# Graph network on one core: the direct products move to the node update's PSUM bank, builds get a fourth bank and their one-hots a third slot

## The chip, the cores and the metric

The kernel runs on 1 core of one Trainium2 chip. The metric is the device time of that core in microseconds; the median of several executions is compared. Before the change it is 2679.72 us (3 runs, 2676.95 to 2680.86).

## The reference

Two layers of message passing over a graph of 6250 nodes with 64 features and 206250 edges, which are sorted by target `dst`; every node has a loop to itself.

```
h  = relu(layernorm(x))
m  = relu(concat(h[src], edge_attr) @ W1 + b1) @ W2 + b2        # per edge
a  = segment_sum(m, dst)
x  = x + relu(concat(h, a) @ U1 + c1) @ U2 + c2                 # the node update
h2 = relu(layernorm(x))
out = x + segment_sum(h2[src] * edge_weight, dst)
```

## The kernel before

The edges come in 202 groups of 1024 (8 tiles of 128). Since they are sorted by target, the targets of a tile span at most 6 nodes and those of a group at most 40 (the kernel tests that and has a slow branch for other graphs, which isn't taken here). The nodes are held as 50 blocks of 125, and 5 blocks are a chunk (10 chunks).

**Pass 1** (`fast_groups`, written out by hand on each engine, one step `s` for a group) does two things with each group.

The first is layer 1. POOL gathers the 128 rows of a tile from `table1` by an indirect DMA (L608, 8 for a group), three groups ahead at most (`gather1` waits for `pre_made` of three groups before). TensorE turns the edge features (`turn_ea`, L916) and multiplies them (`make_q`, L923). DVE adds the gathered rows to the product (`add_product`, L1305), makes a one-hot of the targets (`make_hot`, L1310) and adds the sums of the group before to the running sums (`add_sums`, L1318). ACT applies relu (L713), and TensorE sums over the targets (`sum_hid`, L929).

The second prepares layer 2. For each tile TensorE builds a matrix with a row for each node of a block and a column for each of 50 blocks times 6 targets, in which the edge weights stand: a product of two one-hots, the weight split in three bf16 parts (`build_tile`, 3 matmuls of 128x300, L946). DVE makes the one-hots for four tiles at once (`make_quad`, two for a group): one comparison (L1323), four comparisons (L1325) and three multiplies (L1329). Both sides have slots: `hot_eq`, `hot_w` and `hot_key` are there twice, so quad `q` waits until the tiles of quad `q - 2` are built (`tile_built >= 4 (q - 1)`). The products lie in three PSUM banks (`build_bank`, tile `i` waits for `tile_kept` of tile `i - 3`), from which ACT copies them to `tiles` in SBUF (L721, four slots of a group each). DVE makes `make_quad(2s + 2)` and `make_quad(2s + 3)` in step `s`, after `add_product(s)`, `make_hot(s)` and `add_sums(s - 1)`.

A finished group goes to DRAM (SP, L470), and **pass 2** reads it back in pieces of two groups and one or two chunks (`load_piece`, L490) and multiplies it by `h2` (`multiply`, L1032), a batch of two groups after the other (101 batches). The result of a batch is copied by ACT (`keep_u`, L778) and put in its place.

Not all of it waits for pass 2. As soon as the sums of a chunk are complete, its node update is made within pass 1. `SUMMED[c]`, 23 to 202, is the step for it: `make_g` in two halves (L973) in steps SUMMED and SUMMED + 1, `make_up` (L980) in SUMMED + 2, and layer norm on DVE and ACT up to SUMMED + 5. From step `READY[c] = SUMMED[c] + 6` on `h2` of the chunk is known, and batches still to be built multiply it at once (`direct`, L960, half a batch a step, two steps behind). `ready_for(b)` says how many chunks batch `b` takes so. Their sum goes from ACT (`keep_partial`, L729) to DRAM (L476), and their blocks needn't be stored or read again. The direct products have a PSUM bank of their own (`u_bank[0]`); the node update uses `mid_bank`.

Pass 2's loads on SP start when the last `direct_kept` and all stores have landed (`fast_end`).

Of the kernel before, what the change touches and what calls it, by code (L numbers as in the profile page):

```python
# [5 lines left out]
ALU = mybir.AluOpType  # L6
# [8 lines left out]
P = 128  # L15
D = 64
T = 8
# [4 lines left out]
NP = 125  # L22
BLK = 5
# [5 lines left out]
ROUND = 12582912.0  # L29
SLACK = 31.0  # L30
STAGE = 4
SPLIT = 3
PIECES = 10
SLOTS = 4
# [77 lines left out]
def build(nc, x, src, dst, edge_attr, edge_weight, w1, b1, w2, b2, u1, c1, u2, c2, out):  # L112
# [20 lines left out]

    per_group = N * GE / E
    SUMMED = [min(GROUPS, -int(-(CN * (c + 1) + SLACK) // per_group) + 1) for c in range(CHUNKS)]
    READY = [SUMMED[c] + 6 for c in range(CHUNKS)]

    def ready_for(b):

# [20 lines left out]
    with ExitStack() as ctx:  # L160
        def sb(name, shape, dt=F32):
            return ctx.enter_context(nc.sbuf_tensor(name, shape, dt))
# [72 lines left out]

        QW = 2 * P
        KW = 2 * KEYS
        bld = sb("bld", [P, 2 * (QW + PARTS * QW + KW)])
        bld_bf = bld[:, :].bitcast(BF16)
        assert 2 * GROUPS * T <= 2 * (QW + PARTS * QW + KW) and PIECES * 4 * BLK * GC <= STAGE * ROW  # L240

        def quad(at, n):
            return bld_bf[:, 2 * at:2 * at + 4 * n].rearrange("p (e t) -> p e t", t=4)

        hot_eq = [quad(s * QW, P) for s in range(2)]
        hot_w = [[quad(2 * QW + s * (PARTS * QW + KW) + k * QW, P) for k in range(PARTS)] for s in range(2)]
        hot_key = [bld_bf[:, 2 * at:2 * at + 4 * KEYS].rearrange("p (t c) -> p t c", t=4)
                   for at in (2 * QW + PARTS * QW, 2 * QW + 2 * PARTS * QW + KW)]
# [395 lines left out]
        def _(act):  # L644
# [70 lines left out]
            def keep_tile(g, t):  # L715
                i = g * T + t
                if t == 0 and g >= STAGE:
                    act.wait_ge(adj_stored[g % STAGE], 16 * (g // STAGE))
                    wait_count(act, direct_done, direct_upto((g - STAGE) // 2))
                act.wait_ge(tile_built, i + 1)  # L720
                act.copy(tiles[:, g % STAGE, :, t * WT:(t + 1) * WT],  # L721
                         build_bank[i % 3][:, 0:KEYS].rearrange("p (h w) -> p h w", w=WT)).then_inc(tile_kept, 1)

            def keep_partial(b):
                n = direct_upto(b)
                act.wait_ge(direct_done, n)
                if n > 2:
                    act.wait_ge(s_stored[n % 2], 16 * ((n - 1) // 2))
                act.copy(s_stage[:, n % 2, :], u_bank[0]).then_inc(direct_kept, 1)  # L729

            def relu_g(c, half):
                cols = (0, SPLIT * NP) if half == 0 else (SPLIT * NP, CN)
# [11 lines left out]
            def fast_groups():  # L744
                act.wait_ge(table_turned, 20)
                keep_eaT(0, 0, ea_bank)
                keep_eaT(1, 1, ea_bank)
                for s in range(GROUPS + 6):
                    if s < GROUPS:
                        for t in range(3):  # L750
                            keep_tile(s, t)
                        make_hid(s, s % TWO)
                        for t in range(3, T):
                            keep_tile(s, t)
                        if s + 2 < GROUPS:
                            keep_eaT(s + 2, s % TWO, ea_bank)
                    if s % 2 == 1 and s >= 3:
                        b = (s - 3) // 2
                        if b < BATCHES and ready_for(b):
                            keep_partial(b)  # L760
                    for c in range(CHUNKS):
                        if s == SUMMED[c]:
                            relu_g(c, 0)
                        if s == SUMMED[c] + 1:
                            relu_g(c, 1)
                        if s == SUMMED[c] + 2:
                            clear_sums(c)
                        if s == SUMMED[c] + 3:
                            square(2)(c, 0)
                        if s == SUMMED[c] + 4:  # L770
                            root(2)(c, 0)

            def keep_u(b):
# [49 lines left out]
        def _(pe):  # L823
# [115 lines left out]
            def build_tile(g, t):  # L939
                i = g * T + t  # L940
                q, u = i // 4, i % 4
                if u == 0:
                    pe.wait_ge(quad_made, q + 1)
                wait_count(pe, tile_kept, i - 2)
                for k in range(PARTS):
                    last = pe.matmul(build_bank[i % 3][:, 0:KEYS], hot_w[q % 2][k][:, :, u], hot_key[q % 2][:, u, :],  # L946
                                     start=(k == 0), stop=(k == PARTS - 1))
                last.then_inc(tile_built, 1)

            def direct(b, half):  # L950

                many = ready_for(b) * BLK
                low, high = (0, many // 2) if half == 0 else (many // 2, many)
                if half == 0:
                    pe.wait_ge(tile_kept, (2 * b + 2) * T)
                    pe.wait_ge(h2_staged, ready_for(b))
                    wait_count(pe, direct_kept, direct_upto(b) - 1)
                slot = 2 * b % STAGE
                for h in range(low, high):
                    last = pe.matmul(half_of(u_bank[0], h), h2[:, h * D:(h + 1) * D], tiles[0:NP, slot:slot + 2, h, :],  # L960
                                     start=(h < 2), stop=(h >= many - 2))
                if half == 1:
                    last.then_inc(direct_done, 1)

            def make_g(c, half):
                cols = (0, SPLIT * NP) if half == 0 else (SPLIT * NP, CN)
                if half == 0:
                    pe.wait_ge(acc_added, SUMMED[c])
                    wait_count(pe, x1_made, c)
                else:  # L970
                    pe.wait_ge(g_staged, 2 * c + 1)
                for w, of in ((u1a, hT), (w2u, acc1)):
                    last = pe.matmul(mid_bank[0:D, 0:cols[1] - cols[0]], w[:, :],  # L973
                                     of[:, c * CN + cols[0]:c * CN + cols[1]], start=(w is u1a), stop=(w is w2u))
                last.then_inc(g_made, 1)

            def make_up(c):
                pe.wait_ge(g_staged, 2 * c + 2)
                for b in range(BLK):
                    last = pe.matmul(mid_bank[0:NP, b * D:(b + 1) * D], t_stage[:, 0, b * NP:(b + 1) * NP],  # L980
                                     u2_s[:, :], start=True, stop=True)
                last.then_inc(up_made, 1)

            def fast_groups():
# [4 lines left out]
                for s in range(GROUPS + 6):  # L989
# [15 lines left out]
                    if 0 <= b < BATCHES and ready_for(b):  # L1005
                        direct(b, s % 2)
                    for c in range(CHUNKS):
                        if s == SUMMED[c]:
                            make_g(c, 0)
                        if s == SUMMED[c] + 1:  # L1010
                            make_g(c, 1)
                        if s == SUMMED[c] + 2:
                            make_up(c)

            def multiply(b):
# [116 lines left out]
        def _(dve):  # L1132
# [186 lines left out]

            def make_quad(q):  # L1320
                g, t = q // 2, q % 2 * 4
                wait_count(dve, tile_built, 4 * (q - 1))
                dve.tensor_tensor(hot_eq[q % 2], iota_lo[:, :, :], over(lo[:, g, t:t + 4], P), ALU.is_equal).then_inc(eq_made, 1)  # L1323
                for u in range(4):
                    dve.tensor_scalar(hot_key[q % 2][:, u, :], iota_key[:, :], key[:, g, t + u:t + u + 1], None,  # L1325
                                      ALU.is_equal)
                dve.wait_ge(eq_made, q + 1)
                for k in range(PARTS):
                    last = dve.tensor_tensor(hot_w[q % 2][k], hot_eq[q % 2], over(part[k][:, g, t:t + 4], P), ALU.mult)  # L1329
                last.then_inc(quad_made, 1)  # L1330

            def add_up(c, up):
# [7 lines left out]
            def fast_groups():  # L1340
                make_quad(0)
                make_quad(1)
                for s in range(GROUPS + 6):
                    if s < GROUPS:
                        add_product(s, s, q_bank)
                        make_hot(s)
# [3 lines left out]
                        if q < 2 * GROUPS:  # L1350
                            make_quad(q)
                    for c in range(CHUNKS):
                        if s == SUMMED[c] + 3:
                            add_up(c, mid_bank[0:NP, 0:BC])
                            centre(2)(c, 0)
                        if s == SUMMED[c] + 4:
                            variance(2)(c, 0)
                        if s == SUMMED[c] + 5:
                            stage_h2(c, 0)

            def put(b):
# [98 lines left out]
```

## Time and profile before

| | |
|---|---|
| median of 3 runs | 2679.72 us |
| profiled execution | 2659.47 us, its span 2657.7 |
| pass 1's gathers | 63.2 to 2203.6 us |
| pass 2 | 2223 to 2657 us |
| busy | PE 77%, DVE 49%, ACT 37%, POOL 64% |
| TensorE's granted clock, mean | 0.888 |

The span is cut into 40 slices, each digit the busy share of one in tenths. POOL's last busy slice is where pass 1 ends. Until there PE, DVE and ACT are busy less than POOL, and each of them waits at some place in every group, so the busy shares alone don't say who sets the pace.

### The profile page before, as it was taken

How to read it: one execution, taken by the hardware profiler on the slowest of the kernel's cores; microseconds unless marked ns; L12 is line 12 of the kernel's file. 1: busy time of each engine (PE TensorE's matmuls, PEld its weight loads, DVE VectorE, ACT ScalarE, POOL GpSimd, SP SyncE). 2: the span in 40 equal slices, each digit the busy share in tenths (PEclk: the TensorE clock that was granted, in tenths of full speed). 3: DMA queues.
4: the chain of work that ended last, by engine and by line, in shares of the span. 5: the costliest groups of instructions: out<-in, count | busy, mean ns of one | idle time of the engine just before them, and what ended most of it. 6: DMA issues, size and time to landing. Idle time of an engine off the chain costs nothing.

```text
span 2657.7 us, 57208 instructions
## 1 busy us (share of the span) xinstructions
PE 2049.9 (77%) x21651; PEld 1747.1 (66%) x21651; DVE 1311.2 (49%) x4334; ACT 974.0 (37%) x2419; POOL 1691.7 (64%) x1659
## 2 busy tenths in 40 slices
PE   5766666777777877777787777877778878999998
PEld 5555555656665666666666666766666767787886
DVE  6655555555555555556555555555555551111122
ACT  3334344444444444444444444444444441000111
POOL 6777777777777777777777777777777771000000
PEclk9988888888888888888888898889899899999998
DMA  3455444454444444334333333333223226999995
GB/s 88 129 169 173 162 159 159 165 171 140 142 140 148 130 132 135 118 119 127 106 109 113 99 97 94 87 94 85 74 74 82 65 62 240 401 377 384 372 350 163
DMA packets 422423, 414.27 MB, mean 156 GB/s; under 512 B 288562, under 2 KB 374178, under 8 KB 416000
## 3 DMA queue, kind: packets, MB, share of 16 engines
q1 hardware_dynamic: 369348, 354.89, 38.6%
q0 software_dynamic: 52064, 53.17, 8.8%
q8 instruction: 176, 2.88, 0.4%
q10 hardware_dynamic: 732, 2.48, 0.4%
q14 instruction: 103, 0.84, 0.1%
HBM read 258.64 MB, written 151.74 MB: 154 GB/s over the span
## 4 chain that ended last, share of the span: by engine, by line
POOL 62%; issue 19%; PE 9%; DMA 8%; DVE 1%; DVEq 0%; SPq 0%; ACT 0%; POOLq 0%
POOL rows L608 62%; DMA stage<-adjacency 7%; PE pair L1032 5%; PE pair L1039 1%; PE pair L1022 1%; PE pair L1045 1%; PE pair L864 1%; DMA x_all<-in_x_dram 1%; PE pair L852 0%; DVEq L1363 0%; PE pair L960 0%; PE pair L1053 0%; DVE nodes L1368 0%; DVE mean L1140 0%; SPq L490 0%
## 5 line engine op out<-in xcount | busy, mean ns | idle before, releaser
L608 POOL DMA_INDIRECT rows<-table,idx x1616 | 1649.4, 1021 | 512.0 <-issue 492.2
L721 ACT COPY stage<-pair 128x300 f32<-128x300 f32 x1616 | 622.3, 413 | 689.8 <-PE pair L946 687.3
L946 PE MATMUL pair<-bld 128*128 128x300 bf16 x4848 | 813.1, 316 | 4.5 <-DVE bld L1329 4.5
L923 PE MATMUL pair<-w1b,rings 128*128 128x128 f32 x1616 | 307.1, 349 | 530.4 <-DVE rings L1305 530.3
L923 PEld LDWEIGHTS pair<-w1b,rings 128*128 128x128 f32 x1616 | 261.2, 246 | 588.3 <-DVE rings L1305 587.9
L946 PEld LDWEIGHTS pair<-bld 128*128 128x128 bf16 x4848 | 552.2, 120 | 134.7 <-DVE bld L1329 7.9
L1329 DVE TENSOR_TENSOR bld<-bld,part 128x512 bf16<-128x512 bf16 x1212 | 432.4, 410 | 0.0
L1323 DVE TENSOR_TENSOR bld<-iota_lo,lo 128x512 bf16<-128x512 f16 x404 | 172.5, 427 | 471.1 <-PE pair L946 468.3
L1325 DVE TENSOR_SCALAR bld<-iota_key,key 128x300 bf16<-128x300 f16 x1616 | 383.5, 300 | 0.0
L1305 DVE TENSOR_TENSOR rings<-rows,pair 128x512 f32<-128x512 f32 x202 | 138.3, 685 | 461.4 <-DMA rows<-table,idx 461.4
L1032 PE MATMUL pair<-stage,h 125*64 125x96 f32 x5870 | 297.4, 253 | 25.0 <-DMA stage<-adjacency 22.2
L929 PEld LDWEIGHTS pair<-hot,rings 128*65 128x65 f32 x3232 | 289.2, 173 | 14.5 <-DVE hot L1310 1.9
L1032 PEld LDWEIGHTS pair<-stage,h 125*64 125x64 f32 x5870 | 259.9, 139 | 52.1 <-DMA stage<-adjacency 38.6
L713 ACT ACTIVATE rings<-rings 128x512 f32<-128x512 f32 x202 | 128.0, 633 | 423.8 <-DVE rings L1305 423.1
L929 PE MATMUL pair<-hot,rings 128*65 128x40 f32 x3232 | 279.8, 256 | 1.7 <-ACT rings L713 1.7
L960 PE MATMUL pair<-stage,h 125*64 125x96 f32 x4230 | 219.9, 250 | 0.4 <-ACT s_stage L729 0.4
L960 PEld LDWEIGHTS pair<-stage,h 125*64 125x64 f32 x4230 | 187.1, 137 | 29.8 <-issue 29.5
L778 ACT COPY bld<-pair 128x96 f32<-128x96 f32 x101 | 24.0, 238 | 363.4 <-PE pair L1032 363.4
L1377 DVE TENSOR_SCALAR bld<-iota,node_off 128x80 f32<-128x80 f32 x101 | 26.2, 260 | 241.7 <-PE pair L1045 241.7
L916 PE MATMUL pair<-ident,rings 128*128 128x128 f32 x808 | 122.2, 274 | 2.4 <-issue 1.7
L708 ACT COPY rings<-pair 128x512 f32<-128x512 f32 x202 | 118.4, 586 | 14.7 <-PE pair L916 9.9
L916 PEld LDWEIGHTS pair<-ident,rings 128*128 128x128 f32 x808 | 98.4, 141 | 5.9 <-issue 2.0
(131 smaller groups left out, 779.3 us busy)
## 6 DMA issues: line engine op xcount, KB each, us to landing
stage<-adjacency SPq DMA_DIRECT2D x270, 480.0 KB, 9.4
rings<-in_edge_attr_dram SPq DMA_DIRECT2D x202, 256.0 KB
adjacency<-stage SPq DMA_DIRECT2D x28, 1200.0 KB
rows<-table,idx POOLq DMA_INDIRECT x1616
adjacency<-stage SPq DMA_DIRECT2D x20, 1080.0 KB
adjacency<-stage SPq DMA_DIRECT2D x20, 960.0 KB
adjacency<-stage SPq DMA_DIRECT2D x20, 840.0 KB
adjacency<-stage SPq DMA_DIRECT2D x20, 720.0 KB
```

The lines of the kernel that those rows point to most:

```text
L608: pool.indirect_dma_start(out=rows[:, slot, t, :], out_offset=None, in_=table, in_offset=bass.IndirectOffsetOnAxis(ap=idx[:, g, t:t + 1], ...
L721: act.copy(tiles[:, g % STAGE, :, t * WT:(t + 1) * WT], build_bank[i % 3][:, 0:KEYS].rearrange("p (h w) -> p h w", w=WT)).then_inc(tile_ke ...
L916: last = pe.transpose(bank[:, a * P:(a + 1) * P], ea_ring[:, slot, a * P:(a + 1) * P], ident[:, :])
L923: last = pe.matmul(bank[:, a * P:(a + 1) * P], eaT[:, slot, a, :], w1b2[:, :], start=True, stop=True)
L929: last = pe.matmul(out[0:m, 0:W], lhs[:, slot, t, 0:m], hot[:, hot_slot, t, :], start=(t == 0), stop=(t == T - 1))
L946: last = pe.matmul(build_bank[i % 3][:, 0:KEYS], hot_w[q % 2][k][:, :, u], hot_key[q % 2][:, u, :], start=(k == 0), stop=(k == PARTS - 1))
L960: last = pe.matmul(half_of(u_bank[0], h), h2[:, h * D:(h + 1) * D], tiles[0:NP, slot:slot + 2, h, :], start=(h < 2), stop=(h >= many - 2))
L1032: last = pe.matmul(half_of(bank, h), h2[:, h * D:(h + 1) * D], held[:, :, h - low * BLK, :], start=(not begun and h < 2), stop=(h >= NB - 2))
L1305: dve.tensor_tensor(pre[:, slot, :, :], rows[:, place % RING, :, :], bank.rearrange("p (t f) -> p t f", f=D), ALU.add).then_inc(pre_made, 1)
L1323: dve.tensor_tensor(hot_eq[q % 2], iota_lo[:, :, :], over(lo[:, g, t:t + 4], P), ALU.is_equal).then_inc(eq_made, 1)
L1325: dve.tensor_scalar(hot_key[q % 2][:, u, :], iota_key[:, :], key[:, g, t + u:t + u + 1], None, ALU.is_equal)
L1329: last = dve.tensor_tensor(hot_w[q % 2][k], hot_eq[q % 2], over(part[k][:, g, t:t + 4], P), ALU.mult)
```

## The change

Three edits go together, all in pass 1.

1. The direct products move from their own bank to the last 96 columns of the node update's bank (`direct_bank` in `pair[1][:, 1]`). They take turns: `make_g` and `make_up` wait for `direct_kept`, and the direct products wait for `g_staged` and `x1_made` in the steps behind. For this the update starts in an odd step (`UPDATE = SUMMED | 1`) and its parts stand two steps apart: halves in UPDATE and UPDATE + 2, `make_up` in UPDATE + 4, `h2` in UPDATE + 7. READY becomes UPDATE + 8, and the loops have GROUPS + 9 steps instead of GROUPS + 6.
2. The bank that is free becomes a fourth one for builds.
3. The one-hots of a quad get a third slot (`QUADS = 3`), so `make_quad(q)` waits for the tiles of quad `q - 3`.

```diff
-    READY = [SUMMED[c] + 6 for c in range(CHUNKS)]
+    UPDATE = [SUMMED[c] | 1 for c in range(CHUNKS)]
+    READY = [UPDATE[c] + 8 for c in range(CHUNKS)]
...
-        mid_bank = pair[1][:, 1, :]
-        build_bank = [pair[2][:, 0, :], pair[2][:, 1, :], pair[3][:, 0, :]]
+        mid_bank = pair[1][:, 1, 0:SPLIT * NP]
+        direct_bank = pair[1][:, 1, 512 - COLS:512]
+        build_bank = [pair[2][:, 0, :], pair[2][:, 1, :], pair[3][:, 0, :], pair[3][:, 1, :]]
+        BUILDS = len(build_bank)
...
-                wait_count(pe, tile_kept, i - 2)
+                wait_count(pe, tile_kept, i - BUILDS + 1)
...
             def direct(b, half):
...
+                for c in range(CHUNKS):
+                    since = 2 * b + 2 + half - UPDATE[c]
+                    if since in (1, 3):
+                        pe.wait_ge(g_staged, 2 * c + (since + 1) // 2)
+                    if since == 5:
+                        pe.wait_ge(x1_made, c + 1)
...
+            def direct_by(s):
+                b = min((s - 3) // 2, BATCHES - 1)
+                return direct_upto(b) if b >= 0 else 0
...
             def make_g(c, half):
+                wait_count(pe, direct_kept, direct_by(UPDATE[c] + 2 * half))
...
             def make_up(c):
                 pe.wait_ge(g_staged, 2 * c + 2)
+                wait_count(pe, direct_kept, direct_by(UPDATE[c] + 4))
...
-                for s in range(GROUPS + 6):
+                for s in range(GROUPS + 9):
...
-                        if s == SUMMED[c]:
+                        if s == UPDATE[c]:
                             make_g(c, 0)
-                        if s == SUMMED[c] + 1:
+                        if s == UPDATE[c] + 2:
                             make_g(c, 1)
-                        if s == SUMMED[c] + 2:
+                        if s == UPDATE[c] + 4:
                             make_up(c)
...
             def make_quad(q):
                 g, t = q // 2, q % 2 * 4
-                wait_count(dve, tile_built, 4 * (q - 1))
+                wait_count(dve, tile_built, 4 * (q - QUADS + 1))
```

The steps of ACT (`relu_g`, `clear_sums`, `square`, `root`) and DVE (`add_up`, `centre`, `variance`, `stage_h2`) move with those of TensorE, and all uses of `% 2` and `% 3` for the slots become `% QUADS` and `% BUILDS`.

## Rows read from the trace of the kernel before

**Rows 1.** The page's chain that ended last, shares of the span by engine.
```profile
POOL 62%; issue 19%; PE 9%; DMA 8%; DVE 1%; DVEq 0%; SPq 0%; ACT 0%; POOLq 0%
```

**Rows 2.** Waits: engine, line, releaser: us in total, times, longest us.
```profile
POOL rows L608 <- issue: 492.2, 1615, 0.3
...
DVE bld L1323 <- PE pair L946: 468.3, 395, 2.4
DVE rings L1305 <- DMA rows<-table,idx: 461.4, 148, 6.0
```

**Rows 3.** The gathers: durations min/median/max in ns; then busy us, mean ns.
```profile
L608 POOL DMA_INDIRECT rows<-table,idx x1616: 940/944/2608, 63.2 to 2203.6; - x180
...
L608 POOL DMA_INDIRECT rows<-table,idx x1616 | 1649.4, 1021 | 512.0 <-issue 492.2 <-DMA table<-h 19.9
```

**Rows 4.** Timeline (start us, us, instruction [idle before]) of DVE and POOL, 946 to 951.
```profile
946.00 0.69 DVE L1305 TENSOR_TENSOR rings<-rows,pair 128x512 f32<-128x512 f32 x1 [1.22 <-DMA rows<-table,idx]
948.32 0.43 DVE L1323 TENSOR_TENSOR bld<-iota_lo,lo 128x512 bf16<-128x512 f16 x1 [0.88 <-PE pair L946]
949.50 1.08 DVE L1329 TENSOR_TENSOR bld<-bld,part 128x512 bf16<-128x512 bf16 x3
...
948.21 0.95 POOL L608 DMA_INDIRECT rows<-table,idx  x1 [0.30 <-issue]
949.47 1.94 POOL L608 DMA_INDIRECT rows<-table,idx  x1 [0.30 <-issue]
```

**Rows 5.** Timeline of DVE and POOL, 1013 to 1015.
```profile
1013.62 1.09 DVE L1329 TENSOR_TENSOR bld<-bld,part 128x512 bf16<-128x512 bf16 x3
...
1013.11 0.99 POOL L608 DMA_INDIRECT rows<-table,idx  x1 [0.30 <-issue]
1014.41 1.12 POOL L608 DMA_INDIRECT rows<-table,idx  x1 [0.30 <-issue]
```

**Rows 6.** Timeline of DVE and POOL, 1825 to 1833.
```profile
1825.65 0.69 DVE L1305 TENSOR_TENSOR rings<-rows,pair 128x512 f32<-128x512 f32 x1 [3.52 <-DMA rows<-table,idx]
1827.97 0.42 DVE L1323 TENSOR_TENSOR bld<-iota_lo,lo 128x512 bf16<-128x512 f16 x1 [1.13 <-PE pair L946]
...
1827.04 0.94 POOL L608 DMA_INDIRECT rows<-table,idx  x1 [0.31 <-issue]
1829.53 1.18 POOL L608 DMA_INDIRECT rows<-table,idx  x1 [0.30 <-issue]
1832.27 1.26 POOL L608 DMA_INDIRECT rows<-table,idx  x1 [0.30 <-issue]
```

**Rows 7.** Timeline of PE, ACT and SP's queue at the end of pass 1.
```profile
2212.50 2.04 PE L960 MATMUL pair<-stage,h 125*64 125x96 f32 x44 [0.42 <-ACT s_stage L729]
2215.60 2.14 PE L960 MATMUL pair<-stage,h 125*64 125x96 f32 x44
2217.78 0.24 ACT L729 COPY s_stage<-pair 128x96 f32<-128x96 f32 x1 [1.51 <-PE pair L960]
2219.62 4.65 SPq L490 DMA_DIRECT2D stage<-adjacency  x9
2223.59 0.75 PE L1032 MATMUL pair<-stage,h 125*64 125x96 f32 x6 [3.23 <-DMA stage<-adjacency]
```

**Rows 8.** Windows: length; busy of PE, PEld, DVE, ACT, POOL; PEclk, DMA share, GB/s.
```profile
2223.00:2600.00 377.00, 354.68 (x6061) 307.64 (x6063) 54.98 (x252) 37.00 (x164) 0.00 (x0) 0.98 1.03 379
```

**Rows 9.** Timeline of DVE, 999 to 1004.
```profile
999.95 0.69 DVE L1305 TENSOR_TENSOR rings<-rows,pair 128x512 f32<-128x512 f32 x1 [1.76 <-DMA rows<-table,idx]
...
1000.96 0.19 DVE L1318 TENSOR_TENSOR nodes<-nodes,pair 65x40 f32 x1
1003.56 0.43 DVE L1323 TENSOR_TENSOR bld<-iota_lo,lo 128x512 bf16<-128x512 f16 x1 [2.42 <-PE pair L946]
```

**Rows 10.** ACT's copy of a batch's result, first and last of two stretches of pass 2.
```profile
L778 ACT COPY bld<-pair x14: 238/238/239, 2230.3 to 2310.6; 128x96 f32<-128x96 f32 x14
...
L778 ACT COPY bld<-pair x11: 238/238/239, 2603.0 to 2626.3; 128x96 f32<-128x96 f32 x11
```

More of the change, by code:

```diff
@@ L31 @@
 STAGE = 4
+QUADS = 3
 SPLIT = 3
@@ L237, in build @@
         KW = 2 * KEYS
-        bld = sb("bld", [P, 2 * (QW + PARTS * QW + KW)])
+        bld = sb("bld", [P, QUADS * (QW + PARTS * QW + KW)])
         bld_bf = bld[:, :].bitcast(BF16)
-        assert 2 * GROUPS * T <= 2 * (QW + PARTS * QW + KW) and PIECES * 4 * BLK * GC <= STAGE * ROW
+        assert 2 * GROUPS * T <= QUADS * (QW + PARTS * QW + KW) and PIECES * 4 * BLK * GC <= STAGE * ROW
         def quad(at, n):
             return bld_bf[:, 2 * at:2 * at + 4 * n].rearrange("p (e t) -> p e t", t=4)
-        hot_eq = [quad(s * QW, P) for s in range(2)]
-        hot_w = [[quad(2 * QW + s * (PARTS * QW + KW) + k * QW, P) for k in range(PARTS)] for s in range(2)]
+        QUAD = QW + PARTS * QW + KW
+        hot_eq = [quad(s * QUAD, P) for s in range(QUADS)]
+        hot_w = [[quad(s * QUAD + (k + 1) * QW, P) for k in range(PARTS)] for s in range(QUADS)]
         hot_key = [bld_bf[:, 2 * at:2 * at + 4 * KEYS].rearrange("p (t c) -> p t c", t=4)
-                   for at in (2 * QW + PARTS * QW, 2 * QW + 2 * PARTS * QW + KW)]
+                   for at in (s * QUAD + (PARTS + 1) * QW for s in range(QUADS))]
         wgt = bld[:, 0:GROUPS * T].rearrange("p (g t) -> p g t", t=T)
@@ L721, in keep_tile @@
                 act.copy(tiles[:, g % STAGE, :, t * WT:(t + 1) * WT],
-                         build_bank[i % 3][:, 0:KEYS].rearrange("p (h w) -> p h w", w=WT)).then_inc(tile_kept, 1)
+                         build_bank[i % BUILDS][:, 0:KEYS].rearrange("p (h w) -> p h w", w=WT)).then_inc(tile_kept, 1)
             def keep_partial(b):
@@ L728, in keep_partial @@
                     act.wait_ge(s_stored[n % 2], 16 * ((n - 1) // 2))
-                act.copy(s_stage[:, n % 2, :], u_bank[0]).then_inc(direct_kept, 1)
+                act.copy(s_stage[:, n % 2, :], direct_bank).then_inc(direct_kept, 1)
             def relu_g(c, half):
@@ L761, in fast_groups @@
                     for c in range(CHUNKS):
-                        if s == SUMMED[c]:
+                        if s == UPDATE[c]:
                             relu_g(c, 0)
-                        if s == SUMMED[c] + 1:
+                        if s == UPDATE[c] + 2:
                             relu_g(c, 1)
-                        if s == SUMMED[c] + 2:
+                        if s == UPDATE[c] + 3:
                             clear_sums(c)
-                        if s == SUMMED[c] + 3:
+                        if s == UPDATE[c] + 5:
                             square(2)(c, 0)
-                        if s == SUMMED[c] + 4:
+                        if s == UPDATE[c] + 6:
                             root(2)(c, 0)
@@ L943, in build_tile @@
                     pe.wait_ge(quad_made, q + 1)
-                wait_count(pe, tile_kept, i - 2)
+                wait_count(pe, tile_kept, i - BUILDS + 1)
                 for k in range(PARTS):
-                    last = pe.matmul(build_bank[i % 3][:, 0:KEYS], hot_w[q % 2][k][:, :, u], hot_key[q % 2][:, u, :],
+                    last = pe.matmul(build_bank[i % BUILDS][:, 0:KEYS], hot_w[q % QUADS][k][:, :, u], hot_key[q % QUADS][:, u, :],
                                      start=(k == 0), stop=(k == PARTS - 1))
@@ L958, in direct @@
                 slot = 2 * b % STAGE
+                for c in range(CHUNKS):
[4 more added lines that the diff above has]
+                        pe.wait_ge(x1_made, c + 1)
                 for h in range(low, high):
-                    last = pe.matmul(half_of(u_bank[0], h), h2[:, h * D:(h + 1) * D], tiles[0:NP, slot:slot + 2, h, :],
+                    last = pe.matmul(half_of(direct_bank, h), h2[:, h * D:(h + 1) * D], tiles[0:NP, slot:slot + 2, h, :],
                                      start=(h < 2), stop=(h >= many - 2))
@@ L988, in fast_groups @@
                 make_q(0, 0, q_bank)
-                for s in range(GROUPS + 6):
+                for s in range(GROUPS + 9):
                     if s < GROUPS:
@@ L1007, in fast_groups @@
                     for c in range(CHUNKS):
-                        if s == SUMMED[c]:
+                        if s == UPDATE[c]:
                             make_g(c, 0)
-                        if s == SUMMED[c] + 1:
+                        if s == UPDATE[c] + 2:
                             make_g(c, 1)
-                        if s == SUMMED[c] + 2:
+                        if s == UPDATE[c] + 4:
                             make_up(c)
@@ L1321, in make_quad @@
                 g, t = q // 2, q % 2 * 4
-                wait_count(dve, tile_built, 4 * (q - 1))
-                dve.tensor_tensor(hot_eq[q % 2], iota_lo[:, :, :], over(lo[:, g, t:t + 4], P), ALU.is_equal).then_inc(eq_made, 1)
+                wait_count(dve, tile_built, 4 * (q - QUADS + 1))
+                dve.tensor_tensor(hot_eq[q % QUADS], iota_lo[:, :, :], over(lo[:, g, t:t + 4], P), ALU.is_equal).then_inc(eq_made, 1)
                 for u in range(4):
-                    dve.tensor_scalar(hot_key[q % 2][:, u, :], iota_key[:, :], key[:, g, t + u:t + u + 1], None,
+                    dve.tensor_scalar(hot_key[q % QUADS][:, u, :], iota_key[:, :], key[:, g, t + u:t + u + 1], None,
                                       ALU.is_equal)
@@ L1328, in make_quad @@
                 for k in range(PARTS):
-                    last = dve.tensor_tensor(hot_w[q % 2][k], hot_eq[q % 2], over(part[k][:, g, t:t + 4], P), ALU.mult)
+                    last = dve.tensor_tensor(hot_w[q % QUADS][k], hot_eq[q % QUADS], over(part[k][:, g, t:t + 4], P), ALU.mult)
                 last.then_inc(quad_made, 1)
@@ L1342, in fast_groups @@
                 make_quad(1)
-                for s in range(GROUPS + 6):
+                for s in range(GROUPS + 9):
                     if s < GROUPS:
@@ L1352, in fast_groups @@
                     for c in range(CHUNKS):
-                        if s == SUMMED[c] + 3:
+                        if s == UPDATE[c] + 5:
                             add_up(c, mid_bank[0:NP, 0:BC])
                             centre(2)(c, 0)
-                        if s == SUMMED[c] + 4:
+                        if s == UPDATE[c] + 6:
                             variance(2)(c, 0)
-                        if s == SUMMED[c] + 5:
+                        if s == UPDATE[c] + 7:
                             stage_h2(c, 0)
```

1 line of the change is left out of this document (added).

## Prediction

> **What bounds the kernel now.** I read the chain of work that ended last first. 62% of it is POOL at L608, the gathers of pass 1, and 19% is "issue" [rows 1]. The waits of POOL come next: before 1615 of the 1616 gathers it sat idle 492.2 us in total and never over 0.3 us at a time [rows 2]. So no gather ever waited for another engine. POOL issues one after the other from 63.2 to 2203.6 us [rows 3], and that stretch is as long as 1616 gathers of 1.02 us with 0.30 between them. The other engines follow. DVE waits 461.4 us for gathered rows and 468.3 us for TensorE's builds [rows 2]. Whatever gives PE, ACT or DVE slack in pass 1 doesn't shorten it; only a shorter gather does.
>
> The gathers' durations hold the one thing that can move. Their median is 944 ns, their mean 1021 [rows 3]: 1649.4 - 1616 x 0.944 = 124 us are stretch, 0.61 us for each of 202 groups. The rows side by side show what stretches them. At 949.47 a gather takes 1.94 us, and at 949.50 DVE begins three L1329 multiplies that last 1.08 [rows 4]. At 1013.62 the same three begin 0.51 us into a gather, and the price is 0.05 in that one and 0.18 in the next [rows 5]. The two builds begun from 1827.97 on cost 0.24 and 0.32 [rows 6]. The price of a four-tile build on DVE thus lies between 0 and 1.0 us, and depends on where in the gather's 1.25 us period it falls. The number of these instructions doesn't change with the edit. Their places do.
>
> After pass 1 two more stages count: the seam to pass 2 [rows 7], and pass 2, where the DMA engines are busy throughout from 2223 to 2600 us (share 1.03, 379 GB/s) [rows 8].
>
> **Part 1: third slot for the one-hots.** `make_quad(2s+2)` waited for tile 3 of the group in hand, which TensorE builds only after `make_q`. It now waits for all tiles of the group before, which are long built. Today the first L1323 starts 2.3 us after its group's L1305 (946.00 to 948.32, 0.88 of it waiting for PE) [rows 4], or 3.6 us (999.95 to 1003.56) where PE is slower [rows 9]. Without the wait it follows L1318, which ends 1.2 us after L1305's start (999.95 to 1001.15) [rows 9]. The second L1323 needs tile 3, which is there at 2.3 to 3.6 us, before DVE asks at 1.2 + 2.45 = 3.65. So nearly all pairs should stand 2.45 us apart, beginning 1.2 us after L1305. DVE's own gain (part of 468.3 us of waiting) is worth nothing, since it then waits longer for rows.
>
> The price of a pair: of the 201 pairs, 99 already stand 2.45 us apart. I took for each of them the stretch of six gathers from the one in which its first L1323 starts, and set it against the place of that start in the gather's period. A start at 0.09 to 0.15 us costs 1.0 (25 pairs; 948.32 lies 0.11 into the gather of 948.21 [rows 4]). At 0.30 to 0.56 it costs 0.14 (15 pairs), at 0.56 to 0.80 0.30 (7), at 0.80 to 1.04 0.58 (16; 1827.97 lies 0.93 into the gather of 1827.04 [rows 6]), at 1.04 to 1.25 0.67 (31), at 0 to 0.09 0.56 (4). The mean over the 99 is 0.625. Then I asked of each of 190 groups where in the period the moment 1.2 us after its L1305 lies: 12 at 0 to 0.09, 6 at 0.09 to 0.15, 17 at 0.15 to 0.30 (one pair there cost 0.30; I take 0.15), 47, 31, 24 and 53 in the four bins behind. The sum is 6.7 + 6.0 + 2.6 + 6.5 + 9.4 + 14.0 + 35.4 = 80.6 us, or 0.424 a group. The dear place loses most of its members, because 1.2 and 2.3 us lie on different sides of the period. The other operations of a group stretch its gathers by some 0.05 us by the same count, and that stays. So 201 x 0.424 + 10 = 95, and 3 for the gathers before the first group, 98 us of stretch where 124 are now: 26 us less. The places are those of today's landings, which the new order shifts as well (a stored group goes out at another moment, and rows behind it land later), so I take two thirds: **-18 us**. Bounds: -40 (every pair at 0.36) and +30 (every pair at 0.70, the price just behind 1.04).
>
> The Trainium skill has a rule for this, "SBUF — State Buffer", section "SBUF: two separate sides": VectorE and GpSimd share a port pair that is an exclusive lock, held for a whole instruction, and descriptors that GpSimd writes wait for it. The rows agree that there is a block (1.94 us at 949.47), but most of L1329's time costs nothing: 404 x 1.05 = 424 us of multiplies go with 124 of stretch. What it would make of the change is the second rival.
>
> **Part 2: fourth build bank.** `build_tile` waits for the tile four back instead of three. ACT's copies and PE's builds aren't on POOL's path: nothing. The cover is PE's wait for rows; if that were gone, this would be a gain and no cost.
>
> **Part 3: shared bank, later node update.** The direct products now wait after each half of the node update, and `make_g` and `make_up` wait for `direct_kept`. Queued behind these waits are the next group's builds and `make_q`, hence `hid`, and DVE's L1305 two steps on. It is at most three waits for each of 10 chunks. POOL sees L1305 only through `pre_made` of three groups before, so two groups of (2203.6 - 63.2) / 202 = 10.6 us stand in between: nothing, up to a delay of some 17 us.
>
> READY moves from SUMMED + 6 to (SUMMED | 1) + 8. From SUMMED = 23, 43, 63, 83, 103, 123, 143, 164, 184 the sum of `ready_for` falls from 423 to 412: one batch later for seven chunks, two for two. Eleven times 5 blocks of 2 groups (240 KB) are stored and read again, and multiplied in pass 2. There a batch takes (2310.6 - 2230.3) / 13 = 6.18 us with 10 chunks to load and (2626.3 - 2603.0) / 10 = 2.33 with 2 [rows 10]: 0.48 for each. 11 x 0.48 = **+5.3 us**. Bytes alone give 11 x 246 KB / 379 GB/s = 7.1; if the late ones hide in PE's own chain it is 4. The extra stores in pass 1 (2.7 MB in 2100 us) cost nothing beside a half idle DMA.
>
> **Part 4: the seam.** Pass 2's loads (2219.62) wait for the last partial product to be kept and stored. Today `make_g` stands between its halves; it moves behind. The halves run from 2212.50 and 2215.60 [rows 7], the second at once behind the first's 2.04: 2214.5 instead of 2215.6, **-1.1 us**. The node update ends about 1 us later, but only the last piece of batch 0 needs it, and that is far behind the first landing at 2223.59. The bounds are -1.1 and +1.
>
> **Sum.** -18 + 5.3 - 1.1 = -13.8 us on the profiled execution (2659.5, span 2657.7): 0.52%. On the median, 20 us above the profiled one, 2679.7 x 0.9948 = 2666.
>
> **Rivals.** A, the forecast: the pairs leave the dear place. 2666, with its own range 2655 to 2675.
> B: the stretch stays what it is. For it: all instructions remain, and half the pairs already stand 2.45 apart without being cheaper than the rest. It is also what the skill's rule gives, where every overlap blocks for its length. Against it are the 25 pairs at 1.0, whose start the edit removes. +5.3 - 1.1 = +4.2: 2684.
> C, slower: pairs begin just before the end of a period. Rows that land 1.4 us after the last gather (late in pass 1, as at 1825.65) put L1323 at about 1.06, where a pair costs 0.7. It decides if the mean pair costs over (124 - 13) / 201 = 0.55. With 0.70 throughout it is 201 x 0.15 = +30, with half of that +15 + 4.2 = +19: 2699. For it: 53 of 190 stand there already by my count, and early traffic that now scatters the landings may thin.
> D, slower: the bank's turns hold up TensorE by more than the two groups, and POOL waits. The waits are short (a copy of 0.24 us [rows 7]); were it 5 us for each of 10 chunks, 2730.
> That the third slot frees nothing, since DVE finds another wait, falls together with B.
>
> **Chances.** A 0.56, B 0.20, C 0.20, D 0.04. The measurement tells apart about 0.2%, 5.4 us: 2674 to 2685 is "same". A gives faster 0.49 and same 0.07; B same 0.12, slower 0.07 and faster 0.01; C and D slower. Faster 0.50, same 0.20, slower 0.30. The range runs from the deeper bound of part 1 (2648) to C at half weight (2697).
>
> **What would show it.** L608's mean falls from 1021 to about 1010 ns at the same median (each 1% is 16 us); L1323's waiting for PE falls from 468 us to under 100, while L1305's waiting for rows grows by as much. A gather of 1.94 us gets rare. POOL's idle stays at 0.3 at most; if not, it is D. The first load of pass 2 comes 1.6 us after the end of the last L729, as now (2217.78 + 0.24 to 2219.62), and L1032 has 110 more records (5980) with pass 2 some 5 us longer. If L608's mean is 1021 again, B; if over 1030, C. The prediction is wrong above all if the starts of L1323 don't fall where today's landings put them.

## The result, and the profile after

The change makes the kernel slower: 2897.68 us (median of 4, 2884.36 to 2918.09) beside 2680.29. The ratio is 1.082, 95% interval 1.0756 to 1.0885. The forecast was 2666 us in a range of 2648 to 2697. The profiled execution took 2918.09 us, its span 2916.3: 258.6 more than the span before.

The waits and the gathers' group of the changed kernel, in the form of [rows 2] and [rows 3] (L617 is L608 of before, L1327 is L1305, L1345 is L1323):

```profile
DVE rings L1327 <- DMA rows<-table,idx: 1183.5, 200, 9.4
...
POOL rows L617 <- issue: 492.2, 1615, 0.3
...
DVE bld L1345 <- PE pair L955: 27.1, 111, 0.7
```
```profile
L617 POOL DMA_INDIRECT rows<-table,idx x1616: 940/944/5042, 63.3 to 2459.4; - x180
...
L617 POOL DMA_INDIRECT rows<-table,idx x1616 | 1904.9, 1179 | 512.1 <-issue 492.2
```

POOL still waits for nobody: 492.2 us in 1615 pieces of at most 0.3, to the digit as in [rows 2]. The median of a gather is still 944 ns. What grew is the busy time, 1649.4 to 1904.9 us. These 255.5 us are all but 3 of the 258.6. By the reckoning of the prediction (1904.9 - 1616 x 0.944) the stretch is now 379 us, where it was 124. The longest gather takes 5.04 us.

Here is one of the long ones. First DVE, then POOL, start and duration in us (L1332 is the one-hot of the targets, L1340 the sums, L1347 and L1351 the comparisons and multiplies of a quad):

```profile
1001.35 0.69 DVE L1327 TENSOR_TENSOR rings<-rows,pair 128x512 f32<-128x512 f32 x1 [2.36 <-DMA rows<-table,idx]
...
1002.47 0.41 DVE L1345 TENSOR_TENSOR bld<-iota_lo,lo 128x512 bf16<-128x512 f16 x1
1002.80 0.91 DVE L1347 TENSOR_SCALAR bld<-iota_key,key 128x300 bf16<-128x300 f16 x4
1003.64 1.08 DVE L1351 TENSOR_TENSOR bld<-bld,part 128x512 bf16<-128x512 bf16 x3
1004.64 0.41 DVE L1345 TENSOR_TENSOR bld<-iota_lo,lo 128x512 bf16<-128x512 f16 x1
1004.98 0.91 DVE L1347 TENSOR_SCALAR bld<-iota_key,key 128x300 bf16<-128x300 f16 x4
1005.81 1.09 DVE L1351 TENSOR_TENSOR bld<-bld,part 128x512 bf16<-128x512 bf16 x3
```
```profile
1002.65 1.19 POOL L617 DMA_INDIRECT rows<-table,idx  x1 [0.30 <-issue]
1004.14 3.58 POOL L617 DMA_INDIRECT rows<-table,idx  x1 [0.30 <-issue]
1008.02 0.94 POOL L617 DMA_INDIRECT rows<-table,idx  x1 [0.30 <-issue]
```

The gather begins at 1004.14, amid the first quad's multiplies. It ends at 1007.72, 0.82 us after the last multiply of the second quad (1006.90). In the kernel before, the gather of 949.47 [rows 4] was caught in the same way, and this is what stood behind its multiplies:

```profile
950.78 0.43 DVE L1323 TENSOR_TENSOR bld<-iota_lo,lo 128x512 bf16<-128x512 f16 x1 [0.20 <-PE pair L946]
951.12 0.92 DVE L1325 TENSOR_SCALAR bld<-iota_key,key 128x300 bf16<-128x300 f16 x4
951.96 1.09 DVE L1329 TENSOR_TENSOR bld<-bld,part 128x512 bf16<-128x512 bf16 x3
```

It ended at 951.41, 0.83 us after 950.58, where the multiplies ended and DVE waited 0.20 us for TensorE. The gather got through in that short wait, and the second quad cost it nothing. In the group shown from the changed kernel no wait stands there: the second L1345 begins 2.17 us after the first, not 2.45, and the gather waits for both quads. Over the whole trace of the changed kernel 83 of the 201 pairs of quads follow each other so; in the other 118 a pause of about 0.24 us is left in the middle. The pause before the first quad is gone in all 201. The 119 gathers of 1.8 us and more hold 292 us of the stretch, and their median end is 0.82 us after the end of an operation, mostly the last multiply of a quad, behind which VectorE paused.

### The profile page after: what moved, and what is told of

Same layout as the page of the kernel before. It is cut to its first block, busy times and chain, and to the rows that moved or that the text cites. A ratio compares the mean times of both kernels' runs of the same rounds, so it can differ in the third digit from the quotient of the medians.

```text
span 2916.3 us, 57246 instructions
## 1 busy us (share of the span) xinstructions
PE 2116.1 (73%) x21649; PEld 1793.8 (62%) x21649; DVE 1284.4 (44%) x4334; ACT 975.8 (33%) x2418; POOL 1947.2 (67%) x1659
## 4 chain that ended last, share of the span: by engine, by line
POOL 65%; issue 17%; DMA 8%; PE 8%; DVE 1%; DVEq 0%; SPq 0%; ACT 0%; POOLq 0%
POOL rows L617 65%; DMA stage<-adjacency 8%; PE pair L1054 4%; PE pair L1061 1%; PE pair L873 1%; PE pair L1067 1%; PE pair L1044 1%; DMA x_all<-in_x_dram 1%; PE pair L861 0%; DVEq L1385 0%; PE pair L1075 0%; SPq L499 0%; PE pair L975 0%; DVE nodes L1390 0%; DVE mean L1162 0%
## 5 line engine op out<-in xcount | busy, mean ns | idle before, releaser
L617 POOL DMA_INDIRECT rows<-table,idx x1616 | 1904.9, 1179 | 512.1 <-issue 492.2
L932 PE MATMUL pair<-w1b,rings 128*128 128x128 f32 x1616 | 342.8, 378 | 709.3 <-DVE rings L1327 709.0
L955 PE MATMUL pair<-bld 128*128 128x300 bf16 x4848 | 837.2, 322 | 4.5 <-DVE bld L1351 4.5
L932 PEld LDWEIGHTS pair<-w1b,rings 128*128 128x128 f32 x1616 | 293.4, 272 | 765.7 <-DVE rings L1327 765.4
L1327 DVE TENSOR_TENSOR rings<-rows,pair 128x512 f32<-128x512 f32 x202 | 138.9, 688 | 1183.5 <-DMA rows<-table,idx 1183.5
L955 PEld LDWEIGHTS pair<-bld 128*128 128x128 bf16 x4848 | 560.8, 122 | 148.0 <-issue 8.6
L1351 DVE TENSOR_TENSOR bld<-bld,part 128x512 bf16<-128x512 bf16 x1212 | 438.2, 415 | 0.0
L1347 DVE TENSOR_SCALAR bld<-iota_key,key 128x300 bf16<-128x300 f16 x1616 | 371.3, 292 | 0.0
L1054 PE MATMUL pair<-stage,h 125*64 125x96 f32 x5980 | 300.9, 251 | 25.8 <-DMA stage<-adjacency 23.3
L938 PEld LDWEIGHTS pair<-hot,rings 128*65 128x65 f32 x3232 | 300.8, 179 | 16.8 <-DVE hot L1332 1.4
L1054 PEld LDWEIGHTS pair<-stage,h 125*64 125x64 f32 x5980 | 261.5, 138 | 54.8 <-DMA stage<-adjacency 44.7
L938 PE MATMUL pair<-hot,rings 128*65 128x40 f32 x3232 | 288.8, 260 | 1.2 <-ACT rings L722 1.2
L1345 DVE TENSOR_TENSOR bld<-iota_lo,lo 128x512 bf16<-128x512 f16 x404 | 168.9, 418 | 28.8 <-PE pair L955 27.1
L787 ACT COPY bld<-pair 128x96 f32<-128x96 f32 x101 | 24.0, 238 | 366.0 <-PE pair L1054 366.0
```

The source lines that it names most:

```text
L617: pool.indirect_dma_start(out=rows[:, slot, t, :], out_offset=None, in_=table, in_offset=bass.IndirectOffsetOnAxis(ap=idx[:, g, t:t + 1], ...
L932: last = pe.matmul(bank[:, a * P:(a + 1) * P], eaT[:, slot, a, :], w1b2[:, :], start=True, stop=True)
L938: last = pe.matmul(out[0:m, 0:W], lhs[:, slot, t, 0:m], hot[:, hot_slot, t, :], start=(t == 0), stop=(t == T - 1))
L955: last = pe.matmul(build_bank[i % BUILDS][:, 0:KEYS], hot_w[q % QUADS][k][:, :, u], hot_key[q % QUADS][:, u, :], start=(k == 0), stop=(k = ...
L1054: last = pe.matmul(half_of(bank, h), h2[:, h * D:(h + 1) * D], held[:, :, h - low * BLK, :], start=(not begun and h < 2), stop=(h >= NB - 2))
L1327: dve.tensor_tensor(pre[:, slot, :, :], rows[:, place % RING, :, :], bank.rearrange("p (t f) -> p t f", f=D), ALU.add).then_inc(pre_made, 1)
```

## Theories and experiments

Theory R: a gather that meets VectorE's work on SBUF (a run of operations without a pause) waits until that work is interrupted. Each operation alone costs at most its own length; a run without a pause costs what is left of the run. Theory P, that of the prediction: each burst of multiplies costs by its place in the gather's period, whatever stands between two bursts. The third is that the shared bank and the later node update are the cause.

**The slot alone**, in the kernel before:

```diff
+QUADS = 3
...
-                wait_count(dve, tile_built, 4 * (q - 1))
+                wait_count(dve, tile_built, 4 * (q - QUADS + 1))
```

> The kernel before with the third slot of the one-hots alone. Theory R (an unbroken run of VectorE operations keeps a gather that met it waiting until VectorE's first pause) and theory P (each L1329 burst costs by its place in the gather's period) both say that the slot is the cause: 2880 to 2900 us, the gathers' mean near 1180 ns. If the shared bank and the later node update are the cause, it stays at 2680.

Measured: 2930.38 us, ratio 1.0946 (1.0914 to 1.0978).

```profile
L610 POOL DMA_INDIRECT rows<-table,idx x1616 | 1915.6, 1185 | 510.6 <-issue 492.2
```

The slot is the whole loss, and a little more than the whole change has: the time lies 30 us above the upper end of the expectation. The stretch is 390 us beside 379; the rest of the 33 us between the two medians isn't explained.

**The banks alone**, the changed kernel with two slots:

```diff
-QUADS = 3
+QUADS = 2
```

> The changed kernel with two slots (QUADS = 2), so the shared bank, the fourth build bank and the later node update alone. If the slot is the cause: 2680.3 + 4.2 = 2684.5 us (+5.3 for eleven chunks more in pass 2, -1.1 at the seam), the gathers' mean near 1021 ns. If the bank's turns are the cause: 2880 or more, with POOL waiting.

Measured: 2677.02 us beside 2681.28, ratio 0.9987 (0.9966 to 1.0007).

```profile
L617 POOL DMA_INDIRECT rows<-table,idx x1616 | 1660.3, 1027 | 510.6 <-issue 492.2
```

No loss, no difference that can be told, and POOL waits for nobody. The 2684.5 expected lies just above the interval's end of 2683. The turns in the shared bank cost nothing on the path that can be seen here.

**A pause before each quad.** The changed kernel, in which DVE waits for the end of its own last operation before it starts a quad (`quad_made` for the quad before, `acc_added` for the sums before a first quad):

```diff
             def make_quad(q):
                 wait_count(dve, tile_built, 4 * (q - QUADS + 1))
+                wait_count(dve, quad_made, q)
+                if q >= 4 and q % 2 == 0:
+                    dve.wait_ge(acc_added, q // 2 - 1)
```

> The changed kernel, in which VectorE waits before each quad for the end of its own last operation (a few hundredths of a us without an operation), so that the places of all bursts stay nearly where they are. Theory R: the pause lets POOL in, a gather is never held longer than one quad (about 2.2 us), none takes 3.5 us or more, the stretch falls from 379 us to under 250 and the time to 2770 or less. Theory P: the stretch stays at about 370 us and the time within 15 us of 2898.

Measured: 2650.01 us, ratio 0.9891 (0.9864 to 0.9918).

```profile
L617 POOL DMA_INDIRECT rows<-table,idx x1616: 941/947/2610, 63.3 to 2191.8; - x180
...
L617 POOL DMA_INDIRECT rows<-table,idx x1616 | 1637.0, 1013 | 512.3 <-issue 492.5
```

The same slots, the same operations, 248 us less. The pause between two quads is a tenth of a microsecond (the end of the multiplies of 1008.99 at 1010.07, the next comparison at 1010.17 in the rows below). The stretch fell from 379 to 1637.0 - 1525.5 = 112 us. The longest gather behind the first 100 us takes 2.01 us.

```profile
1008.99 1.08 DVE L1354 TENSOR_TENSOR bld<-bld,part 128x512 bf16<-128x512 bf16 x3
1010.17 0.42 DVE L1348 TENSOR_TENSOR bld<-iota_lo,lo 128x512 bf16<-128x512 f16 x1
```

The time alone doesn't refute theory P, since the places moved too: the first comparison stands 1.32 us behind the addition where it stood 1.11 (medians). The traces do, by the prediction's own count. For each pair of quads, take the stretch over 944 ns of the six gathers from the one in which its first comparison starts:

| kernel | pauses at the pair | pairs | mean stretch, us | mean where the comparison starts 0.80 to 1.04 us into a gather |
|---|---|---|---|---|
| before | before it and in its middle | 201 | 0.55 | 0.56 (42 pairs) |
| changed | in its middle alone | 118 | 1.13 | 1.10 (46) |
| changed | none | 83 | 2.92 | 3.08 (31) |
| changed, with a pause before each quad | before it and in its middle | 201 | 0.52 | 0.49 (28) |

The same place has three prices, and they go with the pauses.

**A pause after every operation** of a group:

```diff
-                                      ALU.is_equal)
-                dve.wait_ge(eq_made, q + 1)
+                                      ALU.is_equal).then_inc(tick, 1)
+                    dve.wait_ge(tick, 6 * q + u + 1)
...
+                    if k < PARTS - 1:
+                        last.then_inc(tick, 1)
+                        dve.wait_ge(tick, 6 * q + k + 5)
```

(and likewise before each quad, as in the experiment before, and after its first comparison, `add_product` and `make_hot`.)

> The changed kernel, in which VectorE waits after every operation of a group for that operation's end. Theory R: no gather is held for longer than one operation of 0.4 us, the stretch falls below the 124 us of before (to some 60), and the time to 2620 to 2660, faster than before. Theory P: VectorE's bursts are still there, only some 0.4 us longer, so the stretch stays at 300 us or more and the time over 2830.

Measured: 2598.39 us, ratio 0.969 (0.9673 to 0.9706), better than both kernels, and better than expected.

```profile
L618 POOL DMA_INDIRECT rows<-table,idx x1616: 941/947/2609, 63.3 to 2139.8; - x180
...
L618 POOL DMA_INDIRECT rows<-table,idx x1616 | 1585.1, 981 | 512.3 <-issue 492.1
```

The stretch is 60 us. Timeline of a quad's multiplies and of the gathers over them:

```profile
999.61 1.35 DVE L1359 TENSOR_TENSOR bld<-bld,part 128x512 bf16<-128x512 bf16 x3
...
999.82 1.04 POOL L618 DMA_INDIRECT rows<-table,idx  x1 [0.30 <-issue]
1001.16 1.15 POOL L618 DMA_INDIRECT rows<-table,idx  x1 [0.30 <-issue]
```

The three multiplies now take 1.35 us instead of 1.08, since each waits for the one before. The gather that starts among them at 999.82 is held 0.1 us, where that of 1004.14 in the changed kernel was held 2.64. Behind the first 100 us (the longest of the view, 2.61 us, starts at 81 us) no gather takes more than 1.27 us, so none is held for longer than an operation of 0.4 us, as theory R expected.

In the executions of the next four kernels everything was slower, the kernel before too (3450.48 us at a granted clock of 0.78 to 0.79, where it had 0.88 to 0.89); what that was isn't known. The expectations:

> The changed kernel with a pause (a wait for the end of VectorE's own last operation) between the two quads of a group alone, none before the first. Theory R: a gather that is caught waits for one of the two runs and not for both: no gather is held for 4.3 us or more (the changed kernel has some of 4.2 to 5.0), the longest is 0.94 + 3.3, and the stretch lies between the 379 us of the changed kernel and the 112 of the one with a pause before every quad: 150 to 300 us, 2690 to 2830 us of time. Theory P (the place of each burst alone): the places are those of the changed kernel, 2880 to 2900.

> The changed kernel with a pause before each quad and between its three multiplies, none among the comparisons. If only the multiplies keep POOL out, it does what the pauses after every operation did: stretch 60 us or little over, 2598 to 2610. If the comparisons keep it out as well, the stretch stays nearer to the 112 us of the kernel with pauses before quads alone: 2620 to 2645.

> The kernel before (two slots, three build banks, early node update) with a pause after every operation of a group on VectorE. If the pauses alone are the gain, POOL's stretch falls from 124 to about 60 and the time to 2615. If the third slot is needed for it, since VectorE's longer quads and its waits for TensorE's builds now last over 10.3 us a group, rows are taken up late, POOL waits for them, and the time stays over 2635.

> The third slot with a pause after every operation, without the shared bank, the fourth build bank and the later node update. The same stretch of 60 us as with them; without their eleven chunks more in pass 2 and with a later seam it is 2594 (+/- 5) beside 2598. If the fourth build bank matters, it is 2610 or more.

Measured: 3417.25, 3577.56, 3699.95 and 3630.49 us, ratios 0.99, 1.0325, 1.0722 and 1.05. The times don't answer their questions, since something else bounds them: the waits of POOL in the last but one, the kernel before with pauses after every operation, name L1306, DVE's addition.

```profile
POOL rows L609 <- DVE rings L1306: 1081.7, 120, 15.5
...
POOL rows L609 <- issue: 474.1, 1495, 1.8
PEld pair L947 <- issue: 452.0, 405, 12.0
```

Only in these four did POOL wait for another engine for more than 0.3 us at a time: for DVE's addition 716 to 1082 us in all. TensorE stood idle there for up to 12 us at a time without a cause that the profile shows. The kernels with more pauses lost time: 1.0722 (1.0651 to 1.0794) in this one. The gathers themselves behaved as everywhere: their stretch is 161, 56, 60 and 52 us. The same four follow once more, beside a kernel before of its usual time, 2672.00 us.

**A pause between the two quads alone** (`if q % 2: dve.wait_ge(quad_made, q)` in the changed kernel):

> The same kernel as the one with a pause only between the two quads of a group, where the kernel before takes its usual 2680 us. Theory R: no gather of 4.3 us or more, stretch 150 to 300 us, 2690 to 2830 us of time. Theory P: 2880 to 2900.

Measured: 2773.54 us, ratio 1.0353 (1.0298 to 1.0408).

```profile
L617 POOL DMA_INDIRECT rows<-table,idx x1616: 940/945/3106, 63.2 to 2331.1; - x180
...
L617 POOL DMA_INDIRECT rows<-table,idx x1616 | 1776.6, 1099 | 512.0 <-issue 492.2
```

The stretch is 251 us: halfway. The longest gather is 3.11, which is 0.94 and one quad of 2.17. The changed kernel's longest, 5.04, is 0.94 and 4.1, nearly the two. So the pause between the quads is worth 379 - 251 = 128 us, and that before the first, put in besides, 251 - 112 = 139. The change had removed the wait before the first quad in every group and that between the quads in 83 of 201.

**Pauses before quads and between multiplies**, none among the comparisons:

> The same kernel as the one with pauses before each quad and between its multiplies. If only the multiplies keep POOL out: stretch 60 us or little over, 2598 to 2610. If the comparisons do as well: nearer to 112 us, 2620 to 2645. In the disturbed executions its gathers had a mean of 979 ns, which speaks for the first.

Measured: 2622.28 us, ratio 0.9812 (0.9785 to 0.9839), at the low end of the second expectation.

```profile
L618 POOL DMA_INDIRECT rows<-table,idx x1616 | 1605.4, 993 | 512.1 <-issue 492.2
```

The stretch is 80 us, where pauses before quads left 112 and pauses everywhere 60. By these differences the pauses between multiplies are worth 32 of the 52 us, those at the comparisons and the other operations 20.

**Every operation with a pause, two slots**, in the kernel before:

> The kernel before with a pause after every operation, two slots. If the pauses alone are the gain: stretch 60 us, 2615. If the third slot is needed for it: POOL waits for L1305 or rows are taken up late, and the time stays over 2635.

Measured: 2599.00 us, ratio 0.9723 (0.9696 to 0.9749).

```profile
L609 POOL DMA_INDIRECT rows<-table,idx x1616 | 1580.8, 978 | 512.1 <-issue 491.6
```

The stretch is 55 us, and the time 16 us below the 2615 expected.

**Every operation with a pause, three slots, no change of banks:**

> The third slot with a pause after every operation, without the shared bank, the fourth build bank and the later node update: 2594 (+/- 5) beside the 2598 of the kernel that has them; 2610 or more if the fourth build bank matters.

Measured: 2596.13 us, ratio 0.9706 (0.968 to 0.9733).

```profile
L611 POOL DMA_INDIRECT rows<-table,idx x1616 | 1581.6, 979 | 512.1 <-issue 491.9
```

The last of them was expected at 2594 +/- 5 and lies there. The three kernels with pauses everywhere have ratios of 0.969, 0.9723 and 0.9706, whose intervals overlap. The third slot adds nothing to the pauses that these intervals (some 7 us to each side) could show, and neither do the fourth bank and the shared one. The gain is the pauses alone.

## Why the prediction was wrong, step by step

**The bound** was right. POOL's gathers set pass 1, no other engine's slack counts, and only the gathers' durations can move. They moved by 255.5 of 258.6 us. The rival in which the shared bank holds TensorE up (D) didn't come: POOL's longest idle is 0.3 us.

**The places of DVE's work** were right in part. The first comparison was to follow 1.2 us after the addition and follows 1.12 (1001.35 to 1002.47). L1345's waits for TensorE were to fall under 100 us and are 27.1. The second comparison was to stand 2.45 us behind the first. It stands at 2.17, or around 2.5 where it had to wait for tile 3 (111 waits). This is the first wrong step: 2.45 was read from pairs of the kernel before, as the length of a quad's work, and 0.2 us of it was a wait for TensorE. In the gather's period 77 of the 201 first comparisons stand at 0.80 to 1.04 us, where 24 of 190 were forecast. This step is small: at the prediction's own prices the places that came would cost 99 us of stretch, where it forecast 81.

**The price of a pair** is the step that failed. 0.625 us was the mean over 99 pairs, laid over new places to give 0.424. Measured by the same count the 201 pairs of the changed kernel cost 1.87 us each in place of 0.424, 376 us in all and not 99. All of the 99 had a pause in their middle (0.11 us or more) and one before them (0.62 or more), since `tile_built` made DVE wait there. A price taken under these pauses doesn't hold without them. The waits on TensorE counted as DVE's loss, worth nothing to remove; they were the moments in which POOL got through. The prediction put down the 1.0 us of 949.47 to the place at which L1323 started. The place has its part: it decides whether a gather is caught, and how much of the work is then left. But how far the hold reaches depends on the pauses, and without them the price has no upper end at 1.0 or at 0.7: the dearest pair of the changed kernel cost 4.1 us. The bound of +30 us (every pair at 0.70) was a bound on a mean within the old pattern. In the new one the mean is 379 / 202 = 1.9 us a group.

**Rival C** had the sign, and its mechanism (pairs at a dear place) was too small by the same step: 2699 us, and 2714 if every pair stood there. That the sign of C came true is thus no confirmation of it. The likeliest case was wrong in sign. The lower end of the range also has a slip: 2679.7 - 40 + 4.2 is 2644 and not 2648, which changes nothing here.

**The rule of the Trainium skill** ("SBUF — State Buffer", section "SBUF: two separate sides"), an exclusive lock that leaves the loser fully blocked, fits the block that the runs show, but not its length. I had read from 424 us of multiplies against 124 of stretch that most overlap is free, and from its "whole instruction" that the spacing doesn't matter. The runs show a hold across instructions: 2.64 us for the gather of 1004.14 (3.58 - 0.94), over some ten operations of at most 0.42. The page states no such run, and here the measurement decides.

**The fourth bank and the shared bank** were costed at nothing, as measured: 0.9987.

**Pass 2** was to last 5.3 us longer. From the first to the last L778, or L787 after, it is 414.3 before and 420.4 after, 6.1 more in these two profiles; the records of L1054, the L1032 of before, are 110 more, as forecast.

```profile
L787 ACT COPY bld<-pair x101: 238/238/239, 2483.4 to 2903.8; 128x96 f32<-128x96 f32 x101
...
L1054 PE MATMUL pair<-stage,h 125*64 125x96 f32 x5980 | 300.9, 251 | 25.8 <-DMA stage<-adjacency 23.3
```

But the kernel with the slot alone, which has the same pass 2 as before, took 418.0 in its profile. Over all profiles beside a kernel before of its usual time, the four with the pass 2 of before take 414.3 to 418.0, mean 416.3, and the six with that of the change 417.5 to 420.4, mean 418.7. That is about 2.4 us more: the sign is right, and the size about half of the term.

**The seam** was to give 1.1 us. From the start of the last gather to the first load it is 16.0 us before (2203.6 to 2219.62) and 14.6 after (2459.4 to 2473.96): 1.4. Over the same ten profiles the means are 17.5 and 14.8. The gain is there, and rather larger than forecast.

```profile
2473.96 86.76 SPq L499 DMA_DIRECT2D stage<-adjacency  x75
```

**The sum** thus was -18 + 5.3 - 1.1, and is 255.5 + 6.1 - 1.4 = 260, beside 258.6 measured. The error of 272 us is in one term, the -18.

## What to carry to other kernels

Where GpSimd issues indirect DMAs and is the bound, look at VectorE's runs without a pause, not at its busy share: a wait that costs VectorE 0.1 us can be what lets a gather through, and taking such waits away cost 8% here. Before a wait is removed, ask what happens in it; a price read between waits doesn't hold without them. And where VectorE has time to spare (it was busy 49% of the span here), a wait for its own last operation, put in on purpose, was worth 3%.

## What the runs showed of the hardware

- A gather is caught about 0.12 us after its start. In the kernel before, behind the first 100 us, DVE was idle or in L1305 at that moment of 791 gathers, and not one of them is stretched by more than 0.03 us, whatever DVE did later in them; a multiply (L1329) was running there in 288, and 283 of them are stretched. In the changed kernel it is none of 1075, and all of 147. Taken 0.5 us after the start, the same count doesn't separate them: 125 of 809 and 197 of 321. So most of the multiplies' time meets no such moment, which is how 424 us of it can go with only 124 of stretch.
- A gather that is caught and waits for the end of a run needs a further 0.82 us from there (1007.72 - 1006.90; 951.41 - 950.58 in the kernel before), which is 0.94 less the 0.12. The hold can be nearly as long as the run: 4.1 us, where the two quads from 1002.47 to 1006.90 last 4.4.
- Two operations of VectorE that follow without a wait overlap in the records by 0.08 us (1002.47 + 0.41 to 1002.80), and a gather didn't get in between. 0.1 us of pause was enough (2916 to 2648 us of span).
- Not each operation holds. In the rows below, of the changed kernel, the gather of 1346.16 ends at 1351.07, 0.83 us after the last multiply (1350.24), though DVE went on without a pause with L1356, an addition of PSUM to SBUF in f32. L1305 and L1327, which add the gathered rows to a product in PSUM in f32, were running 0.12 us into 96 gathers of the kernel before and 143 of the changed one, and none of these is stretched by more than 0.01 us. Whether PSUM or f32 is the reason wasn't tried.

```profile
1349.15 1.09 DVE L1351 TENSOR_TENSOR bld<-bld,part 128x512 bf16<-128x512 bf16 x3
1350.16 0.48 DVE L1356 TENSOR_TENSOR x_all<-x_all,pair 125x320 f32<-125x320 f32 x1
...
1346.16 4.91 POOL L617 DMA_INDIRECT rows<-table,idx  x1 [0.30 <-issue]
```

- Theory R isn't the whole rule. In the kernel before, one of the four L1325 comparisons was running at that moment of 297 gathers, and none was held for more than 0.10 us, though three multiplies followed without a pause. In the changed kernel it is 233 gathers, and 41% of them were held longer, up to 4.08 us. That pauses shorten the hold is shown; why a comparison lets a gather through behind a pause, and often not without one, stays open.
- It also stays open what made the four executions slow in which the kernel before took 3450 us.
